# Weight preparation inside the first stage, half blocks of tokens in the expert stage, and results added up in two regions

## The chip, the core and the metric

The kernel runs on 1 core of one Trainium2 chip. The metric is the device time of one execution in microseconds (us); the time before is the median of 3 runs. The engines are called TensorE or PE (matrix products; PEld is its weight load), VectorE or DVE, ScalarE or ACT, GpSimd or POOL, and SyncE or SP, which issues most transfers.

## The reference

Inputs are x (8 batches of 100 rows of 512), a context of 8 x 361 x 512, a mask of 8 x 100 x 361 and the weights of four blocks. `h` is the residual row; cut to what matters:

```python
# block 1: a decayed scan over the context, averaged: one summary row a batch
xt = ctx @ W_in.T + b_in;  s_t = sigmoid(decay) * s_(t-1) + xt_t
h  = x + layernorm(layernorm(x) + mean_t(s_t @ W_out.T + b_out)) * gamma + beta
# block 2: feed-forward with quantized activations (int8) and ternary weights (-1, 0, 1)
n  = rms_norm(layernorm(h))
h  = h + bit_linear(gelu(bit_linear(n, w1)), w2)
# block 3: cross attention, 16 heads of 32; q and the output by int8 rows and int8 weight rows
q  = w8a8(layernorm(h), wq, bq);  k = ctx @ wk.T + bk;  v = ctx @ wv.T + bv
h  = h + w8a8(softmax(q @ k.T / sqrt(32) + mask) @ v, wo, bo)
# block 4: 8 experts (512 -> 352 -> 512, silu), the best 2 for each row, weighted by a softmax of their two scores
z  = layernorm(h);  out = h + sum_(e in top2) share_e * (silu(z @ w1[e].T + b1[e]) @ w2[e].T + b2[e])
```

## The kernel before, in words

Each engine has its own hand-written program, and semaphores tie them together; the order of the work is the order of the code. There are three stages, between which all engines meet at the semaphore `a_done` (4 arrivals), and a routing part between the second and the third.

**First stage.** The context of each batch is turned into keys (4 chunks, L828) and values (3 chunks, L834), 56 chunks in all, into the big tiles CT (keys) and VS (values). They are spread between the feed-forward of the 8 batches by `beside` (L242): `early`, `mid`, `late` and `last_` name the chunks that PE makes at four places of a pass. A pass of `body(b)` on PE: first product `g1` (L896), early chunks, turning of the quantized hidden row `hq` (L906), mid chunk, second product `g2` (L913), late chunk, turning of the next batch's row (L882), last chunk. ACT applies the gelu (L689); DVE takes the maxima of it (L1289), rounds (L1296 to L1300), finishes the row (L1314), and makes the rows of the batch after the next (`rows`, L1224). GpSimd makes roots (`rsqrt`, L433 to L439) and one half of `hq` (L467). Before the first pass come the summary: PE multiplies with W_in (L860) and W_out (L867), DVE adds the bias into `summ`, which overlays `xq` (L1221), SP writes it to memory (L337) and reads it back for each batch (L349). `rows(0)` waits for that write before it uses `xq` (L1241). The ternary weights are made from chunks of 2048 columns: ACT scales and rounds by adding a large number (`round_chunk`, L634), DVE clamps (L1202) and subtracts (L1203). The statistics of all 8 rows are taken before the first pass (`row_stats`, L1187), one root serves batches 1 to 7 (L475).

**Between the stages.** After `a_done` SP loads the query and output weights (`wst`), the biases and the first two masks (L354 to L360). DVE takes the row maxima of the weights (`projection_scale`, L1502), ACT and DVE round them (L711, L1514), PE turns them (`turn_projection`, L927), ACT and DVE copy them to `wqT`. The first batch's rows are normed (GpSimd L499), scaled and rounded (DVE), turned, multiplied (`queries`, L941), rescaled (`prep_rescale`, L1362) and, on GpSimd, given weight scale and bias (`scale_q`, L502) from tiles that it makes with 8 instructions (L564, L566). PE runs idle products meanwhile (`hold_clock`, L1084).

**Second stage.** For each batch and head: scores (L964, four heads side by side in quarters of the array's rows), mask and maximum on DVE (L1478), exponential on ACT (L744), turning on PE (L972), copy on ACT (L735), and the mixing with the values (L985, four heads side by side in quarters of the output partitions). Hooks by head number put the next batch's queries, the last batch's output projection and routing scores in between. DVE's `steps` (L1522) does `prep_scale(b + 1)` after head 3. In batch 0, DVE rounds the output weights after head 7 (L1482), PE turns them at heads 10 and 13.

**Routing.** For each row the two best experts are found, and its place in each expert's list is counted by products with a triangular matrix. A row is then sent to its two slots in memory (`send`, L532, one indirect transfer for each batch and choice). The routing is done in two lots: batches 0 to 3 inside the last batch of the attention, batches 4 to 7 at the end (L1555 to L1559). The slots of an expert are RB = 7 blocks of 128 rows. A table (L1562 to L1583) then tells for each of NBLK = 20 blocks its place and its expert.

**Third stage.** 20 steps (`blocks`, L250), each of one block of 128 rows and one expert: the rows are loaded (L398), turned (L1121), copied (L1589), multiplied with the first weights, which stand in CT (L1129), biased (L1603), through silu (L801), turned (L1135), copied (L797), multiplied with the second weights, which stand in VS (L1143), scaled by the share (L807) and added to their rows in memory by an indirect transfer that accumulates (L608). At last the sums are copied to the output (L409).

```python
dve.wait_ge(sem("scratch_out"), 16)                       # L1241, in rows(0) only
NBLK = (B * S * TOPK + E * (P - 1)) // P                  # L36
sp.dma_start(out.rearrange("b s d -> (b s) d"), sums_out[0:B * S])   # L409
```

## Time and profile before

| what | us |
|---|---|
| median of 3 runs | 655.86 (654.63 to 660.86) |
| the profiled execution | 650.6 |
| its span in the profile | 648.6 |
| PE busy in it | 545.3 (84%) |
| DVE busy | 359.8 (55%) |
| ACT busy | 268.3 (41%) |
| GpSimd busy | 196.6 (30%) |

The profiled execution is one more execution beside the three runs. Times of the rows below count from the start of its span. The granted clock is a share of 2.4 GHz; it has two levels, 1.2 and 2.4 GHz.

### The profile page before, as it was taken

How to read it: one execution, taken by the hardware profiler on the slowest of the kernel's cores; microseconds unless marked ns; L12 is line 12 of the kernel's file. 1: busy time of each engine (PE TensorE's matmuls, PEld its weight loads, DVE VectorE, ACT ScalarE, POOL GpSimd, SP SyncE). 2: the span in 40 equal slices, each digit the busy share in tenths (PEclk: the TensorE clock that was granted, in tenths of full speed). 3: DMA queues.
4: the chain of work that ended last, by engine and by line, in shares of the span. 5: the costliest groups of instructions: out<-in, count | busy, mean ns of one | idle time of the engine just before them, and what ended most of it. 6: DMA issues, size and time to landing. Idle time of an engine off the chain costs nothing.

```text
span 648.6 us, 10088 instructions
## 1 busy us (share of the span) xinstructions
PE 545.3 (84%) x3344; PEld 331.9 (51%) x3344; DVE 359.8 (55%) x986; ACT 268.3 (41%) x614; POOL 196.6 (30%) x239
## 2 busy tenths in 40 slices
PE   4998859999999999868998998998540899999980
PEld 2553425555555555436776776676430455555540
DVE  3574797767668644277778777777451221222210
ACT  2826631232223212168988677776300222222220
POOL 1002403322332221153355545542705022221221
PEclk9988979999999999979999899897855799999996
DMA  8997723223124000310533123313504244545425
GB/s 319 422 287 296 255 85 114 67 80 130 50 81 146 1 1 0 132 43 14 191 101 113 55 59 113 105 54 103 175 14 122 66 72 93 84 84 98 78 37 133
DMA packets 32553, 72.53 MB, mean 112 GB/s; under 512 B 4032, under 2 KB 19424, under 8 KB 30452
## 3 DMA queue, kind: packets, MB, share of 16 engines
q1 hardware_dynamic: 28088, 63.27, 29.5%
q0 software_dynamic: 4416, 8.63, 8.2%
q8 instruction: 28, 0.46, 0.3%
q14 instruction: 21, 0.17, 0.1%
HBM read 46.20 MB, written 27.33 MB: 113 GB/s over the span
## 4 chain that ended last, share of the span: by engine, by line
PE 54%; DVE 19%; DMA 8%; issue 6%; POOL 5%; SPq 3%; ACT 2%; POOLq 0%; DVEq 0%; ACTq 0%
PE ps L834 10%; PE ps L1143 8%; PE ps L1129 8%; PE ps L828 6%; DMA XR<-in_x 4%; PE ps L913 4%; PE ps L896 4%; PE ps L972 3%; DVE sN L1478 3%; PE ps L1075 2%; POOL slots_in L537 2%; PE ps L985 2%; PE ps L964 2%; ACT hTe L797 1%; POOL g L499 1%
## 5 line engine op out<-in xcount | busy, mean ns | idle before, releaser
L828 PE MATMUL ps<-CT,wkS 128*128 128x364 f32 x224 | 76.8, 493 | 11.8 <-DMA wkS<-in_wk 9.4
L744 ACT ACTIVATE pE<-sN,nmx 100x361 f32<-100x361 f32 x128 | 77.8, 608 | 7.7 <-DVE nmx L1478 7.7
L834 PE MATMUL ps<-wvS,CT 128*121 128x512 f32 x168 | 78.8, 618 | 0.0
L1478 DVE CUSTOM_DVE_ANT_0 sN<-ps,maskS 100x361 f32<-100x361 f32 x128 | 61.9, 531 | 11.6 <-PE ps L964 5.8
L608 POOL DMA_INDIRECT sums_out<-yb,backI x20 | 31.1, 1554 | 109.7 <-ACT yb L807 105.7
L828 PEld LDWEIGHTS ps<-CT,wkS 128*128 128x128 f32 x224 | 43.4, 198 | 37.7 <-issue 14.0
L972 PE MATMUL ps<-ident,pE 100*121 100x100 f32 x384 | 61.0, 287 | 1.4 <-ACT pT L735 1.1
L1143 PE MATMUL ps<-VS,hTe 118*128 x120 | 56.7, 609 | 5.5 <-ACT hTe L797 5.5
L972 PEld LDWEIGHTS ps<-ident,pE 100*121 100x121 f32 x384 | 49.6, 192 | 21.2 <-issue 19.9
L1603 DVE TENSOR_TENSOR hb<-ps,b1B 128x352 f32<-128x352 f32 x20 | 10.5, 525 | 88.3 <-PE ps L1129 88.3
L735 ACT COPY pT<-ps 121x300 f32<-121x300 f32 x128 | 51.7, 405 | 17.2 <-PE ps L972 17.0
L1129 PE MATMUL ps<-CT,xT 128*128 x160 | 53.0, 475 | 2.0 <-DVE xT L1589 2.0
L834 PEld LDWEIGHTS ps<-wvS,CT 128*121 128x121 f32 x168 | 31.4, 192 | 37.0 <-issue 35.8
L1129 PEld LDWEIGHTS ps<-CT,xT 128*128 128x128 f32 x160 | 31.3, 197 | 24.9 <-issue 12.7
L621 ACT ACTIVATE CT<-ps,biases 128x364 f32<-128x364 f32 x32 | 17.8, 560 | 59.2 <-PE ps L828 59.2
L1143 PEld LDWEIGHTS ps<-VS,hTe 118*128 118x128 f32 x120 | 21.1, 189 | 29.3 <-issue 29.3
L964 PE MATMUL ps<-CT,qn 32*100 32x361 f32 x256 | 28.4, 512 | 8.0 <-DVE nmx L1478 6.9
L807 ACT ACTIVATE yb<-ps,share 128x512 f32<-128x512 f32 x20 | 13.7, 687 | 51.7 <-PE ps L1143 51.7
L435 POOL TENSOR_SCALAR tk<-mv 100x1 f32<-100x1 f32 x16 | 10.3, 646 | 67.2 <-DVE mv L1238 33.7
L467 POOL TENSOR_SCALAR hq<-h 100x1024 bf16<-100x1024 f32 x8 | 10.7, 1342 | 65.4 <-DVE h L1296 65.4
L913 PE MATMUL ps<-w2s,hqT 128*100 128x512 fp8e4 x128 | 28.9, 379 | 1.4 <-ACT hqT L697 1.4
L896 PE MATMUL ps<-w1s,xqT 128*100 128x512 fp8e4 x128 | 28.9, 379 | 0.2 <-ACT xqT L667 0.2
(251 smaller groups left out, 951.3 us busy)
## 6 DMA issues: line engine op xcount, KB each, us to landing
slots_in<-zeros SPq DMA_DIRECT2D x8, 1848.0 KB, 8.2
VS<-in_w SPq DMA_DIRECT2D x6, 1024.0 KB, 14.4
CT<-in_ew SPq DMA_DIRECT2D x8, 704.0 KB
VS<-in_ew SPq DMA_DIRECT2D x8, 672.0 KB
xin<-slots_in SPq DMA_DIRECT2D x20, 264.0 KB, 2.8
CT<-in_ctxT SPq DMA_DIRECT2D x7, 728.0 KB, 19.9
ahead<-in_w SPq DMA_DIRECT2D x2, 1024.0 KB, 14.9
sums_out<-XR SPq DMA_DIRECT2D x8, 200.0 KB
```

The source lines that it names most:

```text
L608: g.indirect_dma_start(sums_out, bass.IndirectOffsetOnAxis(backI[:, t:t + 1], 0), yb[:, t % 2, :], None, bounds_check=B * S + P - 1, compu ...
L735: act.copy(pT[0:TC, ht % (2 * HPC)].rearrange("p c s -> p (c s)"), ps[0:TC, 4 + r, 0:NT * S])\
L744: act.activation(pE[0:S, q, 0:T], sN[0:S, q, 0:T], ACT.Exp, scale=-1.0, bias=nmx[0:S, h_:h_ + 1], accum_out=sums[0:S, j, h_:h_ + 1]).then_ ...
L828: mm = pe.matmul(ps[:, at, 0:TP], wkS[:, k, m * P:(m + 1) * P], ctx(b)[:, k * TP:(k + 1) * TP], start=(k == 0), stop=(k == KC - 1))
L834: mm = pe.matmul(ps[0:TC, at, :], ctx(b)[:, k * TP + c * TC:k * TP + (c + 1) * TC], wvS[:, k, :], start=(k == 0), stop=(k == KC - 1))
L896: mm = pe.matmul(ps[0:S, 2 + m, :], xqT[:, k, :], w1q[:, k * FF + m * 512:k * FF + (m + 1) * 512], start=(k == 0), stop=(k == KC - 1))
L913: mm = pe.matmul(ps[0:S, 7, :], hqT[:, k, :], w2q[:, k * D:(k + 1) * D], start=(k == 0), stop=(k == FC - 1))
L964: pe.matmul(ps[0:S, r, 0:T], qn[at, b % 2, g, :], CT[at, b, g * TP:g * TP + T], start=True, stop=True)\
L972: mm = pe.transpose(ps[0:TC, 4 + r, c * S:(c + 1) * S], pE[0:S, h_ % HPC, c * TC:(c + 1) * TC], ident[0:S, 0:S])
L1129: mm = pe.matmul(ps[:, 2 + j, 0:EH], xT[:, j, k, :], CT[:, e, k * EH:(k + 1) * EH], start=(k == 0), stop=(k == KC - 1))
L1143: mm = pe.matmul(ps[:, 7 - j, :], hTe[0:EC, 1 - j, c, :], vs(e)[0:EC, c * D:(c + 1) * D], start=(c == 0), stop=(c == 2))
L1478: dve.tensor_tensor_reduce(out=sN[0:S, q, 0:T], in0=ps[0:S, q, 0:T], in1=maskS[0:S, j, 0:T], scale=-1.0, scalar=3.4e38, op0=ALU.add, op1=A ...
```

## The change

The diff is long; its parts are:

1. **Constants and tables.** Blocks have BR = 64 rows, NBLK = 32, STEPS = 16, and RB = 13 blocks for each expert. The second choices go to rows of their own, from SECOND = 928 on, in `sums_out`.
2. **Start of the first stage.** x is loaded before W_out. The summary's write goes ahead of two weight loads, and `rows(0)` writes into `h` and not into `xq`, so that the wait at L1241 goes. Statistics of batches 3 to 7 move into the passes, and their roots too. The last two chunks of the second ternary weight get a second ACT instruction (`round_back`) and one DVE instruction in place of two.
3. **Query and output weights in the first stage.** Loads after summary row 2, scales after passes 1 and 2, rounding on ACT after 2 and 3, on DVE after 3 and 4, turning in 4 and 5. The rows of batch 0 are normed and rounded after passes 5 and 6, its queries made in pass 7. `scale_q(0, 0)` goes: DVE makes the first queries itself. The mask of batch 0 is loaded into the last row of z, whose place is free once all keys and values are made.
4. **After `a_done`.** PE starts with the scores. GpSimd keeps its 8 constant instructions and the norm of batch 1.
5. **Routing in three lots** (0 to 3, 4 and 5, 6 and 7), with filler products on PE.
6. **Third stage.** A step takes two blocks, each with its expert: two loads, two halves of every product, the second expert's weights copied by DVE to `w1B` and `w2B` so that PE needs one register for the expert.
7. **The output.** Both regions are read to SBUF in two parts (70% and 30%), added on DVE and written.

```diff
+BR = P // 2
+NBLK = (B * S * TOPK + E * (BR - 1)) // BR
+STEPS = NBLK // 2
+RB = -(-B * S // BR)
+SECOND = B * S + P
+FIRST, THEN = 4, 6
+FILL, FILL_LONG = 6, 10
...
+        first_mask = z[:, B - 1, 0:T]
+        SCALES, ROUNDS, HALVES = {1: 0, 2: 1}, {2: 0, 3: 1}, {3: 0, 4: 1}
+        TURNS = {4: 0, 5: 1}
...
+            sp.wait_ge(sem("summ_ready"), 1)
+            sp.dma_start(summ_dram, summ).then_inc(sem("scratch_out"), 16)
             for c in range(2):
                 sp.wait_ge(sem("pe_once"), c + 2)
                 sp.dma_start(stage(1, c + 2), w2[c + 2]).then_inc(sem(f"ahead_in{c}"), 16)
-            sp.wait_ge(sem("summ_ready"), 1)
-            sp.dma_start(summ_dram, summ).then_inc(sem("scratch_out"), 16)
...
                 sp.dma_start(summB[0:S], summ_dram[b].partition_broadcast(S)).then_inc(sem("summ_in"), 16)
+                if b == 2:
+                    sp.wait_ge(sem("ternary"), 2 * NW)
+                    sp.dma_start(wst[:, 0], wq).then_inc(sem("wq_in"), 16)
+                    sp.dma_start(bqS[:], bq).then_inc(sem("wq_in"), 16)
+                    sp.dma_start(wst[:, 1], wo).then_inc(sem("wo_in"), 16)
...
+            sp.wait_ge(sem("k_mm"), B * KC)
+            sp.wait_ge(sem("v_mm"), after(B * NT))
+            sp.dma_start(first_mask[0:S], mask[0]).then_inc(sem("mask_in0"), 16)
...
+            for i, at in enumerate(lin_parts):
+                sp.dma_start(x_lin[:, at], linear(sums_out[0:B * S])[:, at]).then_inc(sem(f"x_in{i}"), 16)
+                sp.dma_start(s_lin[:, at], linear(sums_out[SECOND:SECOND + B * S])[:, at]).then_inc(sem(f"x_in{i}"), 16)
+            for i, at in enumerate(lin_parts):
+                sp.wait_ge(sem("x_taken"), STEPS + i + 1)
+                sp.dma_start(linear(out.rearrange("b s d -> (b s) d"))[:, at], x_lin[:, at]).then_inc(sem("x_kept"), 16)
...
+            def round_back(c):
+                act.wait_ge(sem("w_round"), NW + c + 1 + c % 2)
+                act.activation(stage(1, c), stage(1, c), ACT.Identity, bias=cols[:, C_NMAGIC:C_NMAGIC + 1])\
+                   .then_inc(sem("w_round"), 1)
...
+            def turn_projection(w):
+                pe.wait_ge(sem("wq_b"), (w + 1) * KC)
+                for k in range(KC):
+                    for j in range(KC):
+                        mm = pe.transpose(ps[:, 2 + k // 2, k % 2 * 256 + j * P // 2:k % 2 * 256 + (j + 1) * P // 2].bitcast(BF16),
+                                          wstb[:, j, k * P:(k + 1) * P], identb[:, :])
+                    mm.then_inc(sem("wq_t"), 1)
...
-            hold_clock(WARM[0])
-            pe.wait_ge(sem("xq2b"), 1)
-            turn_rows(xq2b, "xq2_t", 0)
-            for k in range(KC):
-                turn_projection(0, k, ps[:, k])
-            pe.wait_ge(sem("wqT"), KC)
-            queries(0)
-            hold_clock(WARM[1])
             scores(0, 0)
-            hold_clock(WARM[2])
...
                     for k in range(KC):
-                        mm = pe.matmul(ps[:, 2 + j, 0:EH], xT[:, j, k, :], CT[:, e, k * EH:(k + 1) * EH],
-                                       start=(k == 0), stop=(k == KC - 1))
+                        for w, rows in zip((CT[:, e, k * EH:(k + 1) * EH], w1B[:, j, k * EH:(k + 1) * EH]), halves):
+                            mm = pe.matmul(ps[rows, 2 + j, 0:EH], xT[:, j, k, rows], w,
+                                           start=(k == 0), stop=(k == KC - 1))
...
                     for c in range(3):
-                        mm = pe.matmul(ps[:, 7 - j, :], hTe[0:EC, 1 - j, c, :], vs(e)[0:EC, c * D:(c + 1) * D],
-                                       start=(c == 0), stop=(c == 2))
+                        for w, rows in zip((vs(e)[0:EC, c * D:(c + 1) * D], w2B[0:EC, 1 - j, c * D:(c + 1) * D]), halves):
+                            mm = pe.matmul(ps[rows, 7 - j, :], hTe[0:EC, 1 - j, c, rows], w,
+                                           start=(c == 0), stop=(c == 2))
...
             def copy_x(s, j):
                 dve.wait_ge(sem("x_turned"), s + 1)
-                dve.tensor_copy(xT[:, j].rearrange("p k s -> p (k s)"), ps[:, j, :]).then_inc(sem("xT"), 1)
+                dve.tensor_copy(xT[:, j].rearrange("p k s -> p (k s)"), ps[:, j, :])
+                e = block_expert(mybir.EngineType.DVE, s, 1)
+                if s > 1:
+                    dve.wait_ge(sem("h_mm"), s - 1)
+                dve.tensor_copy(w1B[:, j], CT[:, e, 0:KC * EH]).then_inc(sem("xT"), 1)
...
                 if within(s, 0):
+                    es = [block_expert(mybir.EngineType.DVE, s, half) for half in range(2)]
+                    for half, rows in enumerate(halves):
+                        take_x(s, j, es[half], rows, half)
+                    if s > 1:
+                        dve.wait_ge(sem("y_mm"), s - 1)
+                    dve.tensor_copy(w2B[0:EC, j], vs(es[1])[0:EC, 0:3 * D])
                     alone(dve, ("h_mm", s + 1))
+                    for half, rows in enumerate(halves):
+                        ins = dve.tensor_tensor(hb[rows, j], ps[rows, 2 + j, 0:EH], b1B[rows, es[half], :], ALU.add)
+                    ins.then_inc(sem("h_biased"), 1)
...
+            for i, at in enumerate(lin_parts):
+                dve.wait_ge(sem(f"x_in{i}"), 32 * (STEPS // 2) + 32)
+                dve.tensor_tensor(x_lin[:, at], x_lin[:, at], s_lin[:, at], ALU.add).then_inc(sem("x_taken"), 1)
```

## Rows read from the trace of the kernel before

**Rows 1.** The page: the span and the instructions in it.

```profile
span 648.6 us, 10088 instructions
```

**Rows 2.** Windows: length, busy us (count) of each engine, granted clock, DMA share, GB/s.

```profile
0.00:92.00 92.00, 69.83 (x210) 35.87 (x210) 56.88 (x140) 46.19 (x50) 15.28 (x30) 0.95 0.83 293
92.00:268.00 176.00, 173.32 (x700) 94.47 (x700) 113.48 (x215) 46.02 (x72) 42.58 (x68) 0.99 0.19 62
...
460.00:505.00 45.00, 11.59 (x82) 9.12 (x82) 19.28 (x71) 2.64 (x6) 16.38 (x22) 0.56 0.38 111
505.00:634.00 129.00, 121.62 (x416) 68.54 (x416) 31.76 (x100) 33.35 (x61) 29.54 (x19) 0.98 0.44 76
```

**Rows 3.** Timeline of one expert step: start, us, engine, line.

```profile
540.00 2.84 PE L1143 MATMUL ps<-VS,hTe 118*128 x6 [0.22 <-ACT hTe L797]
...
542.68 2.53 PE L1129 MATMUL ps<-CT,xT 128*128 x8
...
545.45 0.53 DVE L1603 TENSOR_TENSOR hb<-ps,b1B 128x352 f32<-128x352 f32 x1 [4.51 <-PE ps L1129]
...
546.01 0.69 DVE L1589 COPY xT<-ps 128x512 f32<-128x512 f32 x1
...
546.19 2.84 PE L1143 MATMUL ps<-VS,hTe 118*128 x6 [0.22 <-ACT hTe L797]
```

**Rows 4.** L1202 alone: duration in ns, min/median/max, first and last start.

```profile
L1202 DVE TENSOR_SCALAR VS<-VS x6: 1193/1220/1237, 37.1 to 83.4; 128x2048 f32<-128x2048 f32 x6
```

**Rows 5.** Timeline of the second stage: products in quarters of the array.

```profile
449.33 0.87 PE L964 MATMUL ps<-CT,qn 32*100 32x361 f32 x8
...
450.93 0.72 PE L985 MATMUL ps<-pT,VS 121*32 121x100 f32 x24
...
451.58 0.92 PE L1075 MATMUL ps<-ident 128*128 128x112 f32 x6
```

**Rows 6.** Timeline of the end: the last two scatters, the output.

```profile
630.96 1.55 POOL L608 DMA_INDIRECT sums_out<-yb,backI  x1 [4.64 <-ACT yb L807]
...
636.57 1.55 POOL L608 DMA_INDIRECT sums_out<-yb,backI  x1 [4.05 <-DMA sums_out<-yb,backI]
641.30 0.60 SPq L409 DMA_DIRECT2D out<-sums_out  x1
```

**Rows 7.** The issues of transfers: KB each, us from issue to landing.

```profile
wst<-in_wo SPq DMA_DIRECT2D x1, 1024.0 KB, 6.9
```

**Rows 8.** Timeline of the handover from the first stage to the second.

```profile
268.17 0.38 PE L924 MATMUL ps<-ones 128*128 128x1 f32 x2 [0.91 <-DVE XR L1314]
...
276.73 0.35 POOL L564 TENSOR_SCALAR swqB<-ones,wsm 128x100 f32<-128x100 f32 x1 [3.71 <-DVE wsm L1507]
...
280.50 0.34 POOL L566 TENSOR_SCALAR bqB<-ones,bqS 128x100 f32<-128x100 f32 x1
...
288.06 0.87 PE L964 MATMUL ps<-CT,qn 32*100 32x361 f32 x8 [0.53 <-POOL qn L506]
...
289.22 2.09 POOL L499 TENSOR_SCALAR g<-XR,mvb,tb 100x512 f32<-100x512 f32 x1 [0.24 <-POOL tb L439]
```

**Rows 9.** Chain that ended last, from 40 to 60 us.

```profile
53.46 8.37 DMA summary_rows<-xq
```

**Rows 10.** Timeline of the first stage: a row of batch 1, turning hq.

```profile
75.94 1.75 DVE L1233 SCALAR_TENSOR_TENSOR y<-XR,rs,summB 100x512 f32<-100x512 f32 x1 [1.98 <-POOL rs L439]
...
140.96 0.87 PE L906 MATMUL ps<-identb,hq 100*128 100x100 bf16 x16
```

**Rows 11.** Waits of PE, 92 to 268 us: in total, times, longest.

```profile
PE ps L906 <- DVE hq L1300: 5.6, 3, 5.0
```

**Rows 12.** Waits of DVE, 92 to 268 us.

```profile
DVE tk L1289 <- ACT h L689: 12.3, 16, 6.1
```

**Rows 13.** Timeline of the tail: the first send after the last slots.

```profile
486.69 1.14 POOL L537 DMA_INDIRECT slots_in<-z,slotI  x1 [11.11 <-DVE slotI L1469]
```

**Rows 14.** Chain that ended last, from 490 to 506 us: the last send.

```profile
496.07 3.55 DMA slots_in<-z,slotI
```

More of the change, by code:

```diff
@@ L250, in blocks @@
         def blocks(body):
-            for s in range(NBLK + 1):
+            for s in range(STEPS + 1):
                 body(s, s % 2, s // 2)
@@ L602, in _ @@
             g.wait_ge(sem("x_kept"), 16 * B)
-            for t in range(NBLK):
+            for t in range(STEPS):
                 g.wait_ge(sem("y_copied"), t + 1)
@@ L690, in _ @@
                                    scale=tk[0:S, 12:13]).then_inc(sem("gelu"), 1)
+                take(early[:1])
                 if not b:
-                    for c in range(2, NW):
-                        round_chunk(1, c)
-                take(early)
+                    round_chunk(1, 2)
+                    round_back(2)
+                    take(early[1:2])
+                    round_chunk(1, 3)
+                    round_back(3)
+                    take(early[2:])
+                else:
+                    if b == B - 1:
+                        turned_x(0)
+                    take(early[1:])
                 for half in range(2):
@@ L898, in _ @@
                     mm.then_inc(sem("g1"), 1)
-                for q in early:
+                for i, q in enumerate(early):
                     chunk(q)
+                    if b == B - 1 and i == 0:
+                        pe.wait_ge(sem("xq2b"), 1)
+                        pe.wait_ge(sem("x2"), after(b))
+                        turn_rows(xq2b, "xq2_t", 0)
+                    if b == B - 1 and i == 1:
+                        queries(0)
                 pe.wait_ge(sem("hq0"), after(b + 1))
@@ L1210, in _ @@
                 summary_sums(b)
-            for c in range(3):
-                ternary(0, c)
+            ternary(0, 0)
+            ternary(0, 1)
             dve.wait_ge(sem("pe_once"), 2)
@@ new lines, in copy_x, with take_x @@
+                e = block_expert(mybir.EngineType.DVE, s, 1)
+                if s > 1:
+                    dve.wait_ge(sem("h_mm"), s - 1)
+                dve.tensor_copy(w1B[:, j], CT[:, e, 0:KC * EH]).then_inc(sem("xT"), 1)
+            def take_x(s, j, e, rows, half):
+                row = bass.ds(C_TOK + e, 1)
+                dve.tensor_copy(share[rows, s:s + 1], xin[rows, j, bass.ds(D + e, 1)])
+                ch(dve.tensor_scalar(vacant[rows, s:s + 1], xin[rows, j, row], 0.0, part[rows], ALU.is_equal, ALU.mult))
+                ins = dve.tensor_scalar(backI[rows, s:s + 1], xin[rows, j, row], vacant[rows, s:s + 1], -1.0,
+                                        ALU.add, ALU.add)
+                if half:
+                    ins.then_inc(sem("x_taken"), 1)
```

452 lines of the change are left out of this document (240 added, 212 removed).

## Prediction

> **What bounds the kernel now.** I read the page first, for the span: 648.6 us [rows 1]. The profiled execution took 650.6 us, 2.0 more than its span, and the median of the runs, 655.86, lies 5.3 above that. All terms below are made against the profiled execution; what I name as the time is the median less their sum. One busy share over the whole span hides stages with different limits, so next came the windows [rows 2]. From 92 to 268 us TensorE (PE) is busy 173.3 of 176 us: the first stage is bound by PE and every instruction added there costs its length. Its start (0 to 92) has 22 us without PE. From 268 to 289 the attention waits to begin. From 460 to 505 PE is busy 11.6 of 45 us at a granted clock of 0.56: a chain of small routing steps. From 505 to 634 run the 20 expert steps, PE-bound again (121.6 of 129). Behind 634 only the last scatters and the copy to the output are left. Then I took the timeline of one expert step, of the handover at 268 and of the tail, and the waits of 92 to 268.
>
> **The expert steps, 20 to 16.** The list of tokens is now cut into blocks of 64 (at most 32 of them instead of 20 of 128), two blocks to a step, so 16 steps. In the trace a step takes 6.19 us, from the products of L1143 at 540.00 to the same at 546.19, and PE goes through it without a hole [rows 3]. Each product of 128 columns becomes two of 64, one for each expert, into the lower and the upper half of the output partitions. What decides everything is whether the two halves run side by side. The trace has no halves, but quarters: L985 issues 24 records of 32 columns, 100 elements each, and the next line starts 0.65 us later [rows 5]. L1143's 6 records of 512 elements take 2.56 us (542.68 less 540.00, less a start of some 0.1), 0.83 ns an element [rows 3]; 24 x 100 at that rate would be 2.0 us, so three ran at once. L964, quarters by rows, puts 8 records of 361 elements into 0.87 us, where 2.4 us would be serial [rows 5]. I take the pair as fully concurrent. Between normal products the next one's start overlaps the last one's end by about 0.17 us; with a change of shape I give that up, twice a step: 0.35 us. A step becomes 6.55 us. 20 x 6.19 = 123.8 against 16 x 6.55 = 104.8, with 0.5 us for a longer first step: -18.5 us. From above, serial halves: the four h products (2.35 us) and three y products (2.56 us) double, the step is 11.1 us, 16 of them 177.6, +53.8 us. From below, nothing lost: 16 x 6.19, -24.8 us.
>
> The Trainium skill ("TensorEngine Tiling (Array Packing)", Key Properties) says that a change of tiling mode drains TensorE, and that tiles then work independently. It gives no time for the drain. The products of L1075 start 0.07 us before the modelled end of L985 [rows 5], so this trace shows no drain longer than the overlap that I priced; were each drain 0.5 us, the step would be 7.2 us and the saving 8 us.
>
> DVE gets two copies a step, 1408 and 1536 elements, which no row shows in this form. L1202 turns 2048 elements of f32 in 1.22 us [rows 4], which gives 0.84 and 0.92 us; by the slower copy out of PSUM (L1589, 512 in 0.69 us [rows 3]) they would be 1.9 and 2.1. I take the first, as source and target are alike. With the split bias (a second 0.5 us) and a second set of three small ones, DVE has some 4.6 us a step, under PE's 6.55. The copy that PE waits for comes last: the products end, bias 2 x 0.5, xT 0.69, w1B 0.84, 2.6 us after the first bias starts (545.45), so at 548.1, where PE wants it at 548.87: hidden by 0.8 us. GpSimd's scatter waits for the one before: 636.57 less 630.96 (the last row but one of that line starts there) is 5.6 us [rows 6], hidden under 6.55.
>
> **The output.** First and second choices now add up in two regions, which are read back (3.28 MB), added on DVE and written (1.64 MB). Before: copy issued at 641.30, span's end 648.6, 7.3 us [rows 1, 6]. After: of the two 1 MB loads at the handover the second lands 6.9 us after its issue and was issued 0.9 after the first [rows 7]: 2.1 MB in 7.8 us, which I split into 2 us and 360 GB/s. The first 70% of both regions are in after 8.5 us, their addition of 2240 elements takes 2.8 us at the rate of L1589, the store of the whole ends 2 + 4.6 us later: about 17.8 us. +10.5 us; bounds +6 (no latency twice) and +14.
>
> **The handover.** The first stage ends at 268.5 (L924) and the first scores (L964) start at 288.06 [rows 8]. In between lie loads of two weights, their scales (L1504), rounding, turning and the first queries. All of this moves ahead of 268.5, and the mask's place (in z, over the weights of keys and values) lets it come before the stage ends. Scores can start at once: -19.4 us. But GpSimd's work for batch 1 isn't moved: after the barrier it still makes 8 constant tiles (L564, L566: 276.73 to 280.84, 4.1 us), then a root (some 0.9) and L499 (2.1 us) [rows 8]. DVE needs this after its fourth mask, some 2.9 us in; GpSimd is through after 7.5. DVE stands 4.6 us in its own queue, 0.4 of which it did before, and masks, exponentials and scores behind it stand too: +4.3. Out of batch 0 go DVE's rounding of the output weights and its turns: -1.4. Sum -16.5; bounds -20 (the stall caught up) and -12.
>
> **The first stage.** Its start: DVE's L1242 waited for the summary rows to be written, a transfer of 8.4 us behind two weight loads [rows 9], of which 5.4 were lost; it now writes elsewhere. Row statistics and one joint root before rows(1) (a wait of 1.98 on GpSimd [rows 10], four statistics of 0.8) go: 5.2. The output weights of the summary come after x, costing some 1.4; and rows(1) can't start before its summary row, behind 2 MB of weights and 1.8 MB of zeros, has landed: 2. -7 us; bounds -9 and -3. Its middle: PE gets 32 turns of 128 columns (L906's 16 of 100 take 0.87 us [rows 10], so 1.1 for 16: 2.2), 4 turns and 17 products for the queries (0.3 and 0.9): +3.4 us. DVE gets the scales (4 x 0.68 + 0.4, twice), roundings (1.4, twice), and a statistic a pass (0.9); ScalarE (ACT) gets 4 x 0.8 us twice, ahead of the gelu, which starts DVE's chain. DVE's slack ahead of its reductions is 12.3 us in 16 waits, 6.1 in one of them; PE waited for DVE's hq 5.6 us, 5.0 in the first pass [rows 11, 12]: elsewhere hq comes just in time. So passes 1 to 4 each come late by 2 to 3 us, of which 0 to 1.6 lies under PE's chunks: 0.6 + 1.5 + 2 + 1 = +5; bounds 1 and 9. Pass 0: two clamps fall away on DVE (2.4), two rounds of 2 us come on ACT, one statistic: +2; bounds -2 and +4. The stage: -7 + 3.4 + 5 + 2 = +3.4; bounds -4 and +11. SP's new loads stand between summary rows and zeros; the wait for the last clamp holds back only summary row 3, wanted a pass later.
>
> **The tail.** Batches 4 and 5 are sent apart, under the waits of the last rows. Four issues instead of eight follow the last slots: 8 began at 486.69, the last at 496.07 and it landed at 499.6 [rows 13, 14], 1.33 us each: -5.3. Filler products keep PE's clock up (0.56 here [rows 2]): about -1, if it rises. Two xin loads and the w1B copy before the first product, and 2 more small DVE instructions: +1.8. -4.5; bounds -9 and 0.
>
> **Sum.** -18.5 + 10.5 - 16.5 + 3.4 - 4.5 = -25.6 us: 625.0 in a profiled execution like this one, 630.3 at the median; I say 630.
>
> **Rivals.** (1) The halves run one after the other: then the same sum has +53.8 for -18.5, in all +46.7: 703 us, slower. It decides from a step of 8.2 us on (25.6 / 16 added to 6.55). For it: no halves in the trace, and f32 products run in two passes, which might queue per half. Against it: the quarters [rows 5]. 5%. (2) The moved work costs the first stage what it frees: DVE and ACT late in the same passes without catching up, +15 instead of +3.4: 642. For it: PE has only 2.7 us free in 176 [rows 2]. Against it: DVE has 62 us free there. 10%. (3) DVE's copies run at L1589's rate and it bounds the step: 1.0 + 2.1 + 1.0 + 0.7 + 1.9 + waits of 0.7 = 7.4 us, +14: 644. 7%. (4) The steps lose nothing and the clock stays up through the tail: -6.3 and -3: 621. 15%. The forecast has the rest, 63%.
>
> **Range and chances.** The forecast's own range is 620 to 638, from terms whose bounds are some 5 us each way and independent. With rivals 2 to 4: 614 to 646. A measurement of this kernel tells about 1%, 6.6 us, from no change, so "faster" is under 649.3: 0.91. Within 1%: 0.04, rivals 2 and 3 together. Slower: 0.05, rival 1.
>
> **What would show it.** Right: h products of about 2.5 us and a period of 6.4 to 6.7 in the expert steps, 16 of them; first scores within 1 us of the barrier, and DVE waiting about 4 to 5 us for g (L499's successor) after the fourth mask; the barrier at 268 to 276; the end of the last scatter to the span's end about 18 us; 4 sends after the last slots. Wrong: a period over 7, a DVE wait in it for its own copies, a barrier past 280, or the final loads at a rate other than 360 GB/s.

## The result, and the profile after

Beside the kernel before on the same chip, the changed kernel took 628.43 us, the median of 4 runs (626.25 to 629.37); the kernel before took 657.15 (4 runs). The ratio is 0.9554, with a 95% interval of 0.9498 to 0.961: faster by 4.5%. Forecast were 630 us and a range of 614 to 646.

The two medians differ by 28.7 us, the two profiled executions by 21.2 (650.6 and 629.37). Both kernels take longer in executions with a lower mean clock of TensorE (PE), and the two profiles stood differently in this: before at 0.930, after at 0.914. So the profiles are compared stretch by stretch, and a second profile of the unchanged kernel (`a_again`) stands beside the first.

| span of the profile, us | before | after | a_again | change (after, a_again) | forecast |
|---|---|---|---|---|---|
| start to the first scores | 288.06 | 272.67 | 273.38 | -15.4, -14.7 | +3.4 - 19.4 = -16.0 |
| first scores to the last send of slots | 208.0 | 211.8 | 207.9 | +3.8, -0.2 | +4.3 - 1.4 - 6.3 = -3.4 |
| last send to the last scatter | 140.5 | 121.7 | 121.8 | -18.8, -18.7 | -18.5 + 1.8 = -16.7 |
| last scatter to the end | 12.0 | 21.4 | 21.0 | +9.4, +9.0 | +10.5 |
| span | 648.6 | 627.6 | 624.1 | -21.0, -24.5 | -25.6 |

The span answers to [rows 1]. The windows of after, by stage, against [rows 2] (length; busy us and count of PE, PEld, DVE, ACT, POOL; granted clock; DMA share; GB/s):

```profile
88.00:272.00 184.00, 177.50 (x753) 96.98 (x753) 130.92 (x259) 57.33 (x88) 50.35 (x83) 0.98 0.35 85
274.00:450.00 176.00, 158.94 (x1849) 120.84 (x1849) 124.31 (x429) 130.71 (x411) 83.34 (x87) 0.89 0.28 89
450.00:494.00 44.00, 29.26 (x142) 20.38 (x142) 24.29 (x98) 3.18 (x8) 16.95 (x23) 0.75 0.39 112
494.00:604.00 110.00, 100.75 (x556) 44.13 (x556) 72.38 (x176) 27.79 (x49) 23.34 (x15) 0.96 0.40 70
```

The first stage is bound by PE as before: 177.5 of 184 us. DVE's 17 us more there lie under it. The routing stretch has 29 us of PE where it had 11.6, 18.3 of it filler (L1088 7.3, L1146 10.9), and its clock is 0.75 for 0.56. The expert steps now lie in a stretch of 110 us, for 129 before.

**One expert step.** Timeline of after, against [rows 3]:

```profile
546.01 0.64 PE L1202 MATMUL ps<-VS,hTe 118*64 x1 [0.22 <-ACT hTe L845]
...
546.01 0.64 PE L1202 MATMUL ps<-w2B,hTe 118*64 118x512 f32 x1
...
546.92 0.89 DVE L1679 COPY w1B<-CT 128x1408 f32 x1
...
548.63 0.46 PE L1187 MATMUL ps<-CT,xT 128*64 x1
...
548.64 0.46 PE L1187 MATMUL ps<-w1B,xT 128*64 128x352 f32 x1
...
548.95 0.96 DVE L1698 COPY w2B<-VS 118x1536 f32 x1
...
552.30 0.64 PE L1202 MATMUL ps<-VS,hTe 118*64 x1 [0.22 <-ACT hTe L845]
```

The two halves start within 0.01 us of each other. From the first y product to the first h product it takes 2.62 us (548.63 less 546.01), where the six products of full width took 2.68 [rows 3]. The period is 552.30 less 546.01, 6.29 us, 0.10 above that of [rows 3]. DVE's two copies take 0.89 and 0.96 us, where [rows 4] gave 0.84 and 0.92. The w1B copy ends at 547.8, 0.8 us ahead of the products that read it.

**The handover.** Timeline of after, against [rows 8]:

```profile
272.23 0.38 PE L1008 MATMUL ps<-ones 128*128 128x1 f32 x2 [0.91 <-DVE XR L1436]
...
272.67 0.87 PE L1025 MATMUL ps<-CT,qn 32*100 32x361 f32 x8
...
275.82 1.54 PE L1025 MATMUL ps<-CT,qn 32*100 32x361 f32 x8 [2.28 <-DVE nmx L1584]
276.95 2.08 POOL L521 TENSOR_SCALAR g<-XR,mvb,tb 100x512 f32<-100x512 f32 x1 [0.24 <-POOL tb L473]
279.07 0.69 DVE L1352 TENSOR_REDUCE tb<-g 100x1 f32<-100x512 f32 x1 [3.40 <-POOL g L521]
...
282.19 0.48 DVE L1366 TENSOR_SCALAR g<-g,tb 100x512 f32<-100x512 f32 x1
```

Scores start 0.44 us behind the barrier. DVE stands 3.40 us for g, which GpSimd makes behind its constants. The second group of scores takes 1.54 us for 0.87: the clock has gone to its half.

**The start of the first stage.** The chain that ended last, from 20 to 80 us:

```profile
21.57 29.03 DMA summB<-in_b_out
...
50.73 5.99 PE ps L915 x8
...
57.46 1.46 DMA summary_rows<-xq
...
```

The write of the summary rows takes 1.46 us instead of 8.37 [rows 9]. But the output weights' bias, now behind x, lands at 50.6, and PE's L915 waits for it.

**The passes.** PE's rows of pass 4 (start, us, line):

```profile
185.85 0.88 PE L988 MATMUL ps<-identb,hq 100*128 100x100 bf16 x16 [1.95 <-DVE hq L1418]
186.57 1.06 PE L939 MATMUL ps<-identb,VS 128*128 128x128 bf16 x16
```

The turns take 1.06 us, as forecast; PE waits 1.95 us for hq, and 1.73 in pass 3. Before, it waited 0.27 in pass 4 and not at all in pass 3.

**The end.** Timeline of after, against [rows 6]:

```profile
606.18 1.55 POOL L645 DMA_INDIRECT sums_out<-yb,backI  x1 [3.98 <-DMA sums_out<-yb,backI]
611.06 0.35 SPq L439 DMA_DIRECT2D XR<-sums_out  x1
...
612.40 1.03 SPq L440 DMA_DIRECT2D z<-sums_out  x1
619.33 3.56 DVE L1711 TENSOR_TENSOR XR<-XR,z 128x2240 f32<-128x2240 f32 x2 [22.79 <-DMA z<-sums_out]
```

The first addition starts 8.3 us after the first load (forecast 8.5), and the span ends 16.5 us after that load (17.8). The addition of 2240 elements takes 2.49 us; the forecast had 2.8, though the rate of L1589 that it names would give 3.0.

**A gap in the tail.** In after, three rows stand out, and the same copy in a_again does not:

```profile
450.70 0.72 PE L1046 MATMUL ps<-pT,VS 121*32 121x100 f32 x24 [0.99 <-issue]
...
457.50 0.49 ACT L829 COPY oTs<-ps 128x400 f32<-128x400 f32 x1 [6.93 <-remote]
...
458.04 1.09 PE L1095 MATMUL ps<-ident,oTs 128*100 128x128 f32 x4 [6.12 <-ACT oTs L829]
```

```profile
451.45 0.49 ACT L829 COPY oTs<-ps 128x400 f32<-128x400 f32 x1 [1.14 <-PE ps L1046]
```

L829 waits for L1046 alone, which had ended at 451.4. In after it is released 6 us later, together with SP's loads behind the same product; "remote" says that the profile found no releaser. This is the 4 us by which the second line of the table differs.

### The profile page after: what moved, and what is told of

Read it like the earlier page. It is cut to its first block, busy times and chain, and to the rows that moved or that the text cites. A ratio compares the mean times of both kernels' runs of the same rounds, so it can differ in the third digit from the quotient of the medians.

```text
span 627.6 us, 10670 instructions
## 1 busy us (share of the span) xinstructions
PE 537.6 (86%) x3520; PEld 318.9 (51%) x3520; DVE 408.9 (65%) x1094; ACT 266.5 (42%) x605; POOL 189.1 (30%) x243
## 4 chain that ended last, share of the span: by engine, by line
PE 45%; DVE 20%; DMA 11%; issue 10%; POOL 5%; SPq 4%; ACT 3%; another core or an unknown queue 1%; DVEq 1%; POOLq 0%; ACTq 0%
PE ps L882 7%; PE ps L1202 6%; PE ps L1033 5%; DMA summB<-in_b_out 5%; PE ps L1187 4%; PE ps L1134 3%; PE ps L876 3%; PE ps L997 3%; PE ps L1025 2%; PE ps L1046 2%; PE ps L970 2%; DMA summB<-summary_rows 2%; DVE sN L1584 2%; DVE tk L1407 2%; DMA sums_out<-yb,backI 2%
## 5 line engine op out<-in xcount | busy, mean ns | idle before, releaser
L876 PE MATMUL ps<-CT,wkS 128*128 128x364 f32 x224 | 76.7, 493 | 9.7 <-DMA wkS<-in_wk 9.7
L1033 PEld LDWEIGHTS ps<-ident,pE 100*121 100x121 f32 x384 | 52.5, 202 | 21.0 <-issue 19.7
L1584 DVE CUSTOM_DVE_ANT_0 sN<-ps,maskS 100x361 f32<-100x361 f32 x112 | 54.0, 531 | 7.0 <-issue 3.5
L645 POOL DMA_INDIRECT sums_out<-yb,backI x16 | 24.9, 1556 | 97.1 <-ACT yb L855 93.1
L1202 PE MATMUL ps<-VS,hTe 118*64 x96 | 44.5, 600 | 4.5 <-ACT hTe L845 4.5
L1187 PE MATMUL ps<-CT,xT 128*64 x128 | 44.0, 490 | 4.4 <-DVE w1B L1679 4.4
L1202 PE MATMUL ps<-w2B,hTe 118*64 118x512 f32 x96 | 44.6, 600 | 0.0
L1187 PE MATMUL ps<-w1B,xT 128*64 128x352 f32 x128 | 44.0, 490 | 0.0
L658 ACT ACTIVATE CT<-ps,biases 128x364 f32<-128x364 f32 x32 | 17.9, 558 | 52.0 <-PE ps L876 52.0
L1701 DVE TENSOR_TENSOR hb<-ps,b1B 64x352 f32<-64x352 f32 x32 | 16.7, 522 | 26.4 <-PE ps L1187 26.2
L1187 PEld LDWEIGHTS ps<-CT,xT 128*64 128x64 f32 x128 | 18.5, 147 | 29.3 <-issue 17.6
L469 POOL TENSOR_SCALAR tk<-mv 100x1 f32<-100x1 f32 x16 | 10.8, 674 | 69.9 <-DVE mv L1304 45.3
L1134 PE MATMUL ps<-ident 128*128 128x112 f32 x174 | 29.4, 311 | 0.0
## 6 DMA issues: line engine op xcount, KB each, us to landing
sums_out<-zeros SPq DMA_DIRECT2D x1, 1600.0 KB, 19.3
```

Of the source, the lines that this page charges most:

```text
L645: g.indirect_dma_start(sums_out, bass.IndirectOffsetOnAxis(backI[:, t:t + 1], 0), yb[:, t % 2, :], None, bounds_check=SECOND + B * S - 1, ...
L876: mm = pe.matmul(ps[:, at, 0:TP], wkS[:, k, m * P:(m + 1) * P], ctx(b)[:, k * TP:(k + 1) * TP], start=(k == 0), stop=(k == KC - 1))
L1033: mm = pe.transpose(ps[0:TC, 4 + r, c * S:(c + 1) * S], pE[0:S, h_ % HPC, c * TC:(c + 1) * TC], ident[0:S, 0:S])
L1134: pe.matmul(ps[:, 6, KC * S:512], ident[:, :], ident[:, 0:512 - KC * S], start=True, stop=True)
L1187: mm = pe.matmul(ps[rows, 2 + j, 0:EH], xT[:, j, k, rows], w, start=(k == 0), stop=(k == KC - 1))
L1202: mm = pe.matmul(ps[rows, 7 - j, :], hTe[0:EC, 1 - j, c, rows], w, start=(c == 0), stop=(c == 2))
```

## The experiments

All have the changed kernel as their base. The kernel before ran beside each group of four: 652.3 us in the first, 655.0 in the second, 658.1 in the third. Medians are compared within a group, ratios (to the kernel before) between groups.

**1. The changed kernel again.**

> The changed kernel once more, as the measure for the runs beside it: 628 us, within 0.5%. In its profile the question is the stretch behind the last turn of the first matrix of the last rows (L1046, 450.7 to 451.4 us in the profile of after), where ScalarE's L829 and SP's L401 were released only at 457.5. If that gap of 6 us belongs to the order of the program (the sends of lots in front of it, a queue), it is there again within half a us. If it was an accident of that execution, it is gone, and the span is some 6 us shorter than 627.6.

626.05 us (ratio 0.9588, 0.9507 to 0.9668), span 624.1. The gap is gone, so it doesn't belong to the order of the program. Of 13 profiles of the changed kernel and its variants, 4 have such a gap of 4 to 6 us between 440 and 458 us; the profile before has none. What makes it was not found.

Another wait shows once it is gone. GpSimd's and PE's rows in a_again:

```profile
456.25 1.04 POOL L576 DMA_INDIRECT slots_in<-z,slotI  x1 [0.30 <-issue]
457.32 1.26 POOL L549 TENSOR_TENSOR xbo<-XR,boB 100x512 f32<-100x512 f32 x1
...
460.10 0.93 PE L1053 MATMUL ps<-ident,z 100*128 100x100 f32 x4 [2.66 <-DVE z L1510]
```

The first lot's eight sends occupy GpSimd from 446.7 to 457.3, and the root L469, whose statistics had been ready at 453.2, starts behind them and L549, at 458.6.

**2. GpSimd's norm ahead of its constants.**

```diff
+            rstd_b(1)
+            norm_x(1)
             g.wait_ge(sem("wq_in"), 32)
...
             g.wait_ge(sem("pool_setup"), CONSTS + HPC + 2 * KC)
-            rstd_b(1)
-            norm_x(1)
```

> GpSimd makes batch 1's norm ahead of its eight constant tiles instead of behind them. Theory (the handover's stall is GpSimd's norm arriving late): the wait of L1352 for g, 3.4 us in after, falls to nothing, the first matrix product of batch 0 (L1366, 282.18) comes 3 to 4 us sooner, TensorE's clock does not fall at 276, and the kernel takes 3 to 5 us less. Rival (the constants are wanted just as early): the wait moves to whoever needs the constant tiles, and the time stays within 1 us.

621.5 us against 626.05. The handover in its timeline:

```profile
272.40 0.87 PE L1025 MATMUL ps<-CT,qn 32*100 32x361 f32 x8
...
276.84 0.69 DVE L1352 TENSOR_REDUCE tb<-g 100x1 f32<-100x512 f32 x1 [1.44 <-POOL g L521]
...
279.95 0.48 DVE L1366 TENSOR_SCALAR g<-g,tb 100x512 f32<-100x512 f32 x1
```

L1366 comes 7.55 us after the first scores, where it came 9.51 after them in a_again: 2.0 us won. DVE's wait is down from 3.40 to 1.44 and not gone, since g now waits for DVE's statistics behind the barrier. The clock falls all the same, to its half by 280 (a part of the expectation that was wrong). The rest of the 4.5 us lies later: from the first scores to L1366 for batch 7 it took 131.2 us against 135.4, and of that 1.2 and 1.5 are batches 1 and 6, which ran with the clock up here and not there. The edit is worth 2 us by its mechanism. The 2 more are in where the clock falls, and they come and go: with the same edit in it, that stretch took 133.3 to 133.5 us in both_first, three_edits and four_and_split, and 131.4 in four_edits.

**3. The output weights of the summary ahead of x.**

```diff
+            sp.dma_start(woutS, wout).then_inc(sem("wout_in"), 16)
+            sp.dma_start(boutB, b_out.partition_broadcast(B)).then_inc(sem("wout_in"), 16)
             for rows in S_PARTS:
                 sp.dma_start(XR[rows], x[rows]).then_inc(sem("x_rows_in"), 16)
-            sp.dma_start(woutS, wout).then_inc(sem("wout_in"), 16)
-            sp.dma_start(boutB, b_out.partition_broadcast(B)).then_inc(sem("wout_in"), 16)
```

> The output weights of the summary and their bias are loaded ahead of the rows of x again, as in the kernel before. Theory (x ahead of them costs the start, where TensorE's L915 waited 4.9 us and then ran at half clock): L915 waits for nothing, y(0) comes at 54 to 56 us instead of 60.5, the barrier near 268 instead of 272.3, the kernel takes 3 to 6 us less. Rival (passes 0 and 1 are bound by the later loads all the same): x lands later and rows(1) or its summary row wait for it, the barrier stays within 1 us of 272.

621.6 us against 626.05. L915 in this kernel, and then in after:

```profile
44.60 3.64 PE L915 MATMUL ps<-ahead,xm 128*8 128x512 f32 x8
```

```profile
50.73 5.98 PE L915 MATMUL ps<-ahead,xm 128*8 128x512 f32 x8 [4.88 <-DMA summB<-in_b_out]
```

It starts 6.1 us sooner and runs at full clock. The first scores start at 266.33 us, 7.0 sooner than in a_again; 1.7 of them are a pass without a clock dip. The profile's end is only 1.2 us sooner. A window of the last batch shows why, here, and then in a_again (length, PE busy and count, granted clock, DMA share, GB/s):

```profile
431.70:441.70 10.00, 10.00 (x68) 0.50 0.21 73
```

```profile
438.80:448.80 10.00, 9.09 (x119) 0.99 0.24 78
```

At the same distance from the batch's start (30 to 40 us), PE has half its clock here and all of it there: 68 instructions in 10 us against 119. This cost 5.3 us from the last L1366 (batch 7) to the last send: 77.7 against 72.4. The 13 profiles fall into such groups: from L1366 (batch 7) to the first send it is 37.6 to 37.9 us in six and 39.4 to 40.1 in six, and from the first lot's last send to the second's first 14.8 to 15.1 in five and 17.9 to 18.0 in four; most of the rest have a gap.

**4. The halves one after the other.**

```diff
-                    for k in range(KC):
-                        for w, rows in zip((CT[:, e, k * EH:(k + 1) * EH], w1B[:, j, k * EH:(k + 1) * EH]), halves):
+                    for half, rows in enumerate(halves):
+                        for k in range(KC):
+                            w = (w1B[:, j, k * EH:(k + 1) * EH] if half else CT[:, e, k * EH:(k + 1) * EH])
```

and the same for the y products.

> In every expert step all products of the first expert's half are issued, and then all of the second's, instead of one of each in turn; nothing else changes. Theory (two halves overlap because neighbours in the queue go to different halves of the array; the engine doesn't look further ahead): h takes 4.7 instead of 2.4 us and y 5.5 instead of 2.8, the period goes from 6.3 to about 11.4 us, and the kernel from 628 to about 700 to 710 us. Rival (the overlap needs no particular order, or the halves gain nothing over one product of 128 columns): the period stays within 0.5 us of 6.3.

644.22 us against 626.05, and neither theory. Timeline of one step:

```profile
558.24 1.50 PE L1204 MATMUL ps<-VS,hTe 118*64 x3 [0.22 <-ACT hTe L845]
559.15 0.64 PE L1204 MATMUL ps<-w2B,hTe 118*64 118x512 f32 x1
559.57 0.59 PE L1204 MATMUL ps<-VS,hTe 118*64 x1
...
560.00 0.59 PE L1204 MATMUL ps<-VS,hTe 118*64 x1
...
560.43 0.59 PE L1204 MATMUL ps<-VS,hTe 118*64 x1
...
560.86 0.46 PE L1188 MATMUL ps<-CT,xT 128*64 x1
560.92 0.59 PE L1204 MATMUL ps<-w2B,hTe 118*64 118x512 f32 x1
...
562.05 0.51 PE L1188 MATMUL ps<-w1B,xT 128*64 128x352 f32 x1
...
565.76 1.50 PE L1204 MATMUL ps<-VS,hTe 118*64 x3 [0.22 <-ACT hTe L845]
```

The six VS records stand ahead of the six w2B records in the program. Yet the first w2B starts at 559.15, while three VS are still to come (559.57, 560.00, 560.43). And the next step's first h product starts at 560.86 with two w2B outstanding. So the halves overlap without being neighbours, and what is lost is a lead. In y the second half starts 0.9 us behind the first (559.15 less 558.24), but the next h products start 2.62 us behind the first y product as before (560.86 less 558.24). In h it starts 1.19 us behind (562.05 less 560.86), and there all of the loss shows: from the first h to the next y product it takes 4.90 us (565.76 less 560.86), in after 3.67 (552.30 less 548.63). The period is 7.52 us, 1.23 above 6.29, and from the last send to the last scatter it makes 141.1 us against 121.8: 19.3, where full serialisation would have cost some 80 (an estimate, 16 times the 5.1 us a step of the expectation). The Trainium skill ("TensorEngine Tiling (Array Packing)", Key Properties) calls tiles independent in loads and products, and the trace agrees. The Trainium skill ("TensorE: Matmul & The Clock Gate", The mechanism) says that products start strictly in program order; these rows differ, 559.15 before 559.57, and the rows decide.

**5. Both edits of 2 and 3.**

> Both edits of the two runs before it at once: GpSimd's norm of batch 1 ahead of its constants, and the output weights of the summary ahead of x. Each alone took 4.5 us off (626.05 to 621.5 and 621.6). They touch stages that lie one behind the other, so they should add up: about 617 us. Rival: what the second gives is lost again where TensorE's clock falls in the attention (the profile of wout_first had its barrier 6.4 us sooner and its end only 1.2 us); then 619 to 622.

623.62 us (619.24 to 624.9), ratio 0.9512: no better than either alone, and above even the rival's 619 to 622. Its profile has the norm's gain (7.55 us from the first scores to L1366) and the early L915. It also has a clock dip in pass 4 (26.82 us) and the slow form of the last batch, 401.74 to 479.47, to the tenth as wout_first. What follows is that 4 runs here can't tell 3 us apart, and the sum of the two edits had to be asked again with more runs (9 and 10).

**6. No fillers.**

```diff
-FILL, FILL_LONG = 6, 10
+FILL, FILL_LONG = 0, 0
```

> The filler products of the tail (L1088, and the 20 records of L1146) are left out. Nothing of the computation changes. Theory (they hardly help: in after they run at half clock themselves up to 482 us, TensorE then idles 3.6 and 1.9 us, and the first products of the steps, L1187, run at half clock all the same, 4.5 to 5.0 us for what takes 2.4 us later): within 1.5 us of 626. Rival (they hold the clock of the small routing products and of the first two steps): 3 to 6 us slower, with the half clock going on into the third or fourth step.

627.48 us, ratio 0.957 (0.9472 to 0.9668) against 0.9588 for the changed kernel: the same. From the last send to the last scatter it takes 122.3 us against 121.8. In that stretch the fillers as they stand bring half a us. They do raise the clock: from 450 to 494 us it is 0.59 here, 0.68 in a_again. Ahead of the last send this profile takes 2.5 us more than a_again (210.4 for 207.9), but after, both_first and wout_first, with the fillers in, take longer still (211.1 to 213.1), so it isn't shown that they help there.

**7. Longer fillers.**

```diff
-FILL, FILL_LONG = 6, 10
+FILL, FILL_LONG = 6, 14
```

> The last stretch of fillers gets 14 products instead of 10 (28 records instead of 20), so that it ends about when the rows of the first block are there (492.5 in after; the fillers ended at 488.9 and each record takes 0.43 us at full clock, so 3.4 us more). Theory (TensorE's clock falls in the idle time in front of the first step and costs its L1187 2.5 us): the first L1187 runs at full clock and the kernel takes 1 to 3 us less. Rival (1.9 us of waiting for the w1B copy are enough for the fall, or the fillers hold back the first turn L1178): no change, or up to 1 us more.

621.34 us, against 627.48 without fillers in the same group. The rows around the first step, here, and then in a_again:

```profile
474.15 14.72 PE L1146 MATMUL ps<-CT,ident 128*128 128x512 f32 x28
...
491.20 0.51 PE L1187 MATMUL ps<-CT,xT 128*64 x1 [1.89 <-DVE w1B L1679]
```

```profile
474.82 11.34 PE L1146 MATMUL ps<-CT,ident 128*128 128x512 f32 x20
489.17 0.63 PE L1178 MATMUL ps<-ident,xin 128*128 128x128 f32 x4 [3.00 <-DMA xin<-slots_in]
491.69 0.84 PE L1187 MATMUL ps<-CT,xT 128*64 x1 [1.89 <-DVE w1B L1679]
```

Here the fillers end where the rows arrive (L1178 starts at 488.71, with no wait), and L1187 takes 0.51 us a record for 0.84. Behind the wait of 1.89 us for the w1B copy alone the clock is up; behind 3.00 and 1.89 it is down. From the last send to the last scatter: 118.1 us, 3.7 less than a_again.

**8. ScalarE's rounds in the middle of the pass.**

```diff
                 if b in TURNS:
                     copy_projection(TURNS[b])
+                if b in ROUNDS:
+                    round_projection(ROUNDS[b])
                 take(mid)
...
                 take(last_)
-                if b in ROUNDS:
-                    round_projection(ROUNDS[b])
```

> ScalarE rounds the query and output projections (four activations of 0.8 us each in passes 2 and 3 of the first stage) in the middle of the pass, behind its copies of the turned hq, instead of at its end, in front of the gelu of the next pass. Theory (these rounds hold up the gelu and with it DVE's chain, so that hq comes late: pass 3 took 25.0 to 26.7 us against 23.1 before, pass 4 25.1 to 26.8 against 22.6): passes 3 and 4 come back to 23 to 24 us each, the first scores come 3 to 5 us sooner (273 to 269), and so the end. Rival (what is late is DVE's own added work, or TensorE's 16 turns themselves): those passes stay within 0.7 us, and TensorE waits for keys that ScalarE now copies late.

622.39 us (618.69 to 625.09), which alone says little. PE's waits for hq in the passes (total, times, longest), here, and then in a_again:

```profile
PE ps L988 <- DVE hq L1418: 5.5, 4, 2.3
```

```profile
PE ps L988 <- DVE hq L1418: 6.1, 4, 2.1
```

Pass 4 loses 0.75 us of its wait for hq (1.20 for 1.95), pass 3 nothing (1.74 for 1.73). The theory falls for most of the lateness: ScalarE's rounds ahead of the gelu are 0.75 of some 3.7 us. That the rest is DVE's own scales, roundings and statistics is what is left, and wasn't shown by a run.

**9 and 10. Three edits, and four.** norm_first, hold_longer and rounds_mid together; then wout_first too.

> norm_first, hold_longer and rounds_mid together, x still ahead of the output weights. By their traces each holds its gain in a stretch of its own: the norm 3.7 us in the first two batches of the attention (h7 marks 37.29 + 18.56 against 39.25 + 19.79 less what the clock took), the longer fillers 3.6 us between the last send and the last scatter (118.1 against 121.8), the rounds 0.5 to 2 us in pass 4. If they add up: 626 less 8 to 9, 617 to 618 us, with the first L1187 at full clock. Rival: TensorE's clock falls at another place and takes 2 to 5 us of it back: 619 to 622.

> The same three, and the output weights of the summary ahead of x. If the earlier barrier (6.4 us in wout_first, 4.7 in both_first) reaches the end: 612 to 614 us. Rival, for which the profiles of wout_first and both_first speak (both lost 5.3 us in the last batch and the tail, with the clock at half from 430 to 442 us): as three_edits or up to 2 us above it.

624.0 us (7 runs, 622.6 to 628.52) and 617.75 (6 runs, 613.09 to 623.83) beside 658.07 for the kernel before: ratios 0.9471 (0.9426 to 0.9517) and 0.9379 (0.9315 to 0.9443). Both missed what was expected: three_edits lies above its 617 to 618 and its rival's 619 to 622, though the kernel before stood at 658.07 in this group and at 652.26 in the first, and by ratios it is 1.2% under a_again; four_edits lies above its 612 to 614. In one group, then, the medians put the output weights ahead of x at 6.25 us. The runs scatter by 6 and 11 us and the two intervals touch, so the size is rough; the rival, which had four_edits no faster than three_edits, falls. The profile of three_edits is of its longest run, and has the slow last batch and a gap of the kind of after. By stretches the edits are there in four_edits: the last send to the last scatter takes 118.07 us, its pass 4 24.39, and L1366 comes 7.55 us after the first scores. In three_edits the first of these is 119.68, the others are the same.

**11. The sends split around a root.**

```diff
-            send(0, FIRST, 1)
+            send(0, FIRST - 1, 1)
             with_bo(B - 1)
             rstd_z(B - 2)
+            send(FIRST - 1, FIRST, 1)
             rstd_z(B - 1)
```

> The four edits, and GpSimd sends three of the first four batches' slots ahead of the output bias and the root of batch 6, and the fourth behind them. Theory (in the profile of a_again the eight sends, 1.33 us each, hold up GpSimd's L549 and L473, and TensorE's L1053 waits 2.7 us for z): the sends of lot 2 begin 1.5 to 3 us sooner after the first lot than in four_edits, and the kernel takes 1 to 3 us less than four_edits. Rival (another chain, DVE's, ends just behind it): within 1 us of four_edits.

617.11 us (614.89 to 620.17) against 617.75: the same. From the first send to the second lot's first it takes 27.67 us where four_edits took 27.70. But four_edits has a gap of 6 us in this stretch, and this profile has the slow last batch instead; of the other profiles with it and without a gap, wout_first and both_first took 27.52 and 27.55. Either way nothing is won. GpSimd's row behind the first six sends shows why:

```profile
451.09 1.29 POOL L549 TENSOR_TENSOR xbo<-XR,boB 100x512 f32<-100x512 f32 x1 [3.48 <-DVE XR L1502]
```

GpSimd, free of sends, now waits 3.48 us for DVE: the wait of a_again was GpSimd's, but DVE's chain ends just behind it. This kernel's ratio, 0.9368 (0.9317 to 0.9419), is the best of all, and four_edits' isn't told from it: both beat the kernel before by 6.2% and the changed kernel (0.9554, 0.9588) by some 2%.

**12. The first region only.**

```diff
+            sp.dma_start(out.rearrange("b s d -> (b s) d"), sums_out[0:B * S]).then_inc(sem("x_kept"), 16)
```

for the loads, the additions and the stores of L439 to L443 and L1711. The second choices' sums are left out, so the output is incomplete.

> The changed kernel with the output path of the kernel before: the first region is copied to the output in one transfer, and the second region (the second choices' sums) is neither read back nor added, so it is missing in the output. Theory (the two-region output costs 16.5 us from the last scatter's landing to the end of the span, where the copy cost 7.3): 9 to 10 us less than the 626 of a_again, about 617. Rival (part of the 16.5 us is the scatters' own landing and stays, or the copy now waits for them longer): less than 6 us.

618.27 us, ratio 0.9398 (0.9338 to 0.9457). The end of its timeline:

```profile
603.18 1.55 POOL L640 DMA_INDIRECT sums_out<-yb,backI  x1 [3.94 <-DMA sums_out<-yb,backI]
607.70 0.55 SPq L438 DMA_DIRECT2D out<-sums_out  x1
```

Its span is 614.6, so 11.4 us lie behind the start of the last scatter, where after and a_again have 21.4 and 21.0. The second region costs 9.6 to 10 us.

## Why the prediction was right, by its own steps

**The expert steps: mechanism right, the size too careful.** The halves run side by side, so rival 1 fell. Even with the halves issued one after the other a step took 7.52 us (run 4), under the 8.2 from which this rival would have decided. The term that was mis-sized is the 0.35 us for changes of shape: the period rose by 0.10 in place of 0.36, to just under the 6.4 to 6.7 named as the sign of being right. 16 x 0.26 is 4.2 us more than forecast. Half of it was given back: the stretch came out at -18.8 for -16.7. What took it is in run 7: the first two steps wait 1.89 and 2.33 us for w1B, and their h products run at half clock. The 1.8 us that I had for all of this left out the clock. Rival 4 (nothing lost in the steps and the clock up through the tail) came true in its first half only. Rival 3 fell: the copies took the fast rate.

**The output: right.** +9.0 to +9.4 for +10.5, and run 12 gives 9.6 to 10.

**The handover: mechanism right, its price too low.** The first scores came 0.44 us behind the barrier. DVE stood for g after the fourth mask, 3.40 us for the 4.6 of the forecast. Run 2 shows the cause by taking 2.0 us of it away. Yet the attention lost more than the +2.9 forecast (4.3 less 1.4). From the first scores to L1366 for batch 7 (L1359 in the kernel before) it took 130.0 us before, 135.2 in after and 135.4 in a_again: +5.2 and +5.4. Of that, 1.8 lie ahead of batch 1's L1366 and 3.0 or more (19.64 and 19.80 for 16.64) between it and batch 2's, though the output weights' work has left that batch. The forecast has no term for the clock: PE idles with DVE and runs at its half from 274 to 291 us. No run isolates this, but the 13 profiles speak for it: with 17 us of half clock in this place, from batch 1's L1366 to batch 2's takes 19.6 to 20.8 us, with 10 to 14 us of it 18.3 to 19.5.

**The first stage: the sum right, two of its steps wrong and of opposite sign.** Rival 2 (+15) fell. The barrier came at 272.2, +4.1 for +3.4. (a) "The output weights of the summary come after x, costing some 1.4": run 3 shows 5 to 7 us. L915 waits 4.9 us, starts on a fallen clock, and y(0) and summary row 1 follow from it. I had counted the transfer and not the product, nor the clock behind the wait. (b) The start was to give -7 and pass 0 +2. By rows(1)'s first instruction (L1299, 73.42 us for 75.94) the start gave -2.5, and by the next g1 product (104.95 for 109.06) pass 0 gave -1.6; PE's wait for hq in it fell from 5.0 to 2.5 us. Together they gave -4.1 for -5: two errors that hide each other, and that is luck. (c) Passes 1 to 4 were to be late by 0.6, 1.5, 2 and 1. Passes 1 and 2 were not late at all (21.59 and 22.14 against 21.58 and 22.14). Passes 3 and 4 took 51.84 together for 45.68: 0.9 is the 16 turns of pass 4 (the other 16 add 0.9 to pass 5), 1.7 a dip of the clock that falls into one or the other (50.15 in first_region_only, 50.17 in wout_first, which have none), and 3.4 the waits for hq. The rounds that ScalarE makes ahead of the gelu were the smaller part of these (run 8). The dip was in no term: without it the lateness, forecast at 5 us for passes 1 to 4, would have been some 3.5.

**The tail: the sends right, the fillers wrong.** With the +2.9 of the handover, -3.4 was forecast for the stretch; it gave -0.2 in a_again and +3.8 in after. Cut at batch 7's L1366, its second part, for which -6.3 was forecast, took 78.0 us before, 72.4 in a_again and 76.7 in after: -5.6, and -1.3 with the gap. So what the stretch missed in a_again is the handover's, above. The last lot's four sends, first to last, span 4.05 us where eight spanned 9.38. The step that failed is "Filler products keep PE's clock up". The clock rose and nothing came of it: the fillers run at half clock themselves at first and stop 3 us before the rows come, and the first h products are at half clock with them or without (run 6). And the clock, which I had only as a gain, is a cost ahead of the tail: 0.89 from 274 to 450 where it had been 0.96 from 289 to 450. Batch 0 starts cold, and the last batch often does.

**The sum** of the profiles, -21.0 and -24.5 for -25.6, is near. The medians' -28.7 is larger because the profile of before, on which my sum was based, was an execution with a high clock, some 6.5 us under the median of the four runs. I had put such a distance (5.3) on both kernels alike, and the changed kernel's profile lay 0.9 above its median. That the sum came so near is in part luck: the steps' 2 us more than forecast and the handover's 2.4 less cancel, as do the two errors of the first stage.

## What to carry to other kernels

Give each half of the array's columns its own small products, issue the two in turns, and price the pair as one product; issued half by half they still overlapped here, but lost 1.23 us a step. Fillers should last until the awaited data is there; 3 us too short they were worth half a us here, and 3 us longer they gave 3.7. When a load is moved, price the instruction that waits for it and what that wait does to the clock, not the transfer. This kernel has clock dips worth 1.7 to 5 us that come and go between executions. In such a case read an edit's effect in its own stretch, from a mark to a mark, before believing a median of four.

## What the hardware showed that was not expected

- Products of one half started ahead of products of the other that stood before them in the program: w2B at 559.15, the fourth VS at 559.57 (run 4).
- Steps that go from pairs of halves to full-width products and back are 0.10 us longer in all than steps of full width alone (6.29 for 6.19).
- Waits of 3.00 and 1.89 us, with 0.63 us of turns between them, came ahead of eight pairs of products at half clock, 0.79 to 0.85 us a record; behind 1.89 alone they took 0.46 to 0.51 (run 7).
- In 4 of 13 profiles, signals of PE between 440 and 458 us reached ScalarE, DVE or SP 4 to 6 us late. The loads of the expert weights and the sends of slots run then. The cause is open.
